# Attention kernel: probability-value products at two places of a step instead of three, and the causal mask of two maxima units moved from TensorE to VectorE

## What is computed

```python
scores = jnp.einsum('bshd,bthd->bhst', q, k) / jnp.sqrt(HEAD_DIM)
causal = jnp.tril(jnp.ones((S, S), dtype=bool))[None, None]
scores = jnp.where(causal, scores, -jnp.inf)
probs = jax.nn.softmax(scores, axis=-1)
out = jnp.einsum('bhst,bthd->bshd', probs, v).reshape(B, S, KEY_DIM)
```

## Time and profile before

| | us |
|---|---|
| median of 3 runs | 1171.12 |
| lowest, highest | 1170.22, 1174.72 |
| the profiled execution | 1182.48 |
| its span, first to last instruction | 1179.3 |
| TensorE busy | 975.2 |
| VectorE busy | 620.9 |
| GpSimd busy | 464.2 |
| ScalarE busy | 446.0 |

### The profile page before, as it was taken

How to read it: one execution, slowest core, us unless ns; L and a number is a source line. 1 busy time by engine, 2 the same in 40 slices (tenths; PEclk the granted TensorE clock), 3 DMA queues, 4 the chain that set the end, 5 groups by cost and what they waited for, 6 DMA issues and landing times. The chain is left out here.

```text
span 1179.3 us, 17823 instructions
## 1 busy us (share of the span) xinstructions
PE 975.2 (83%) x6250; PEld 773.6 (66%) x6250; DVE 620.9 (53%) x1802; ACT 446.0 (38%) x800; POOL 464.2 (39%) x432
## 2 busy tenths in 40 slices
PE   3699999887419999999943489899999739999996
PEld 1466767564319999999941256575666427888885
DVE  5666787956513333333335767776666143353534
ACT  0155555443003333333300045555556314433332
POOL 3453544464523333222345243454243415434232
PEclk9799999897659999999985689999999659999998
DMA  3442212010142323332022552423310010000001
GB/s 129 160 149 95 81 54 92 26 50 10 63 173 95 112 90 111 116 115 94 22 83 69 187 170 77 160 87 112 126 55 28 1 46 1 1 2 18 18 1 36
DMA packets 50023, 91.78 MB, mean 78 GB/s; under 512 B 7328, under 2 KB 22944, under 8 KB 49824
## 3 DMA queue, kind: packets, MB, share of 16 engines
q1 hardware_dynamic: 46880, 82.49, 20.8%
q0 software_dynamic: 3072, 8.39, 2.2%
HBM read 54.55 MB, written 36.31 MB: 77 GB/s over the span
## 5 line engine op out<-in xcount | busy, mean ns | idle before, releaser
L746 ACT ACTIVATE a_probs<-a_ps_b 128x512 f32<-128x512 f32 x320 | 188.1, 600 | 190.2 <-PE a_ps_b L810 186.4
L794 PE MATMUL a_ps_a<-a_k_st,a_q_st 128*128 128x256 f32 (+3 forms) x512 | 204.2, 440 | 26.9 <-DMA a_k_st<-scratch 17.3
L1004 DVE CUSTOM_DVE_ANT_0 a_masked_s<-a_ps_a,a_mask_f 128x512 f32<-128x512 f32 (+1 forms) x256 | 155.2, 621 | 86.6 <-PE a_ps_a L794 80.6
L794 PEld LDWEIGHTS a_ps_a<-a_k_st,a_q_st 128*128 128x128 f32 x512 | 102.5, 203 | 89.6 <-issue 42.6
L475 POOL TENSOR_SCALAR_AFFINE_SELECT a_probs<-a_probs 128x512 f32<-128x512 f32 x128 | 80.9, 646 | 198.3 <-ACT a_probs L746 198.0
L1594 POOL TENSOR_TENSOR w_lo<-w_raw,w_hi 128x2048 fp32r<-128x2048 f32 x16 | 73.9, 4616 | 186.7 <-ACT w_hi L1612 186.7
L810 PE MATMUL a_ps_b<-a_q_less,a_k_st 128*128 128x384 f32 (+3 forms) x512 | 140.2, 337 | 3.0 <-ACT a_probs L746 2.1
L810 PEld LDWEIGHTS a_ps_b<-a_q_less,a_k_st 128*128 128x128 f32 x512 | 91.3, 197 | 28.6 <-ACT a_probs L746 17.8
L1620 ACT ACTIVATE exp_h_hi<-exp_ps_u 128x320 fp32r<-128x320 f32 x128 | 49.2, 437 | 148.4 <-PE exp_ps_u L1684 148.4
L834 PE MATMUL a_ps_pv<-a_probs,a_v 128*32 128x512 f32 (+3 forms) x1024 | 94.9, 470 | 10.7 <-POOL a_probs L475 10.7
L1649 DVE SCALAR_TENSOR_TENSOR exp_h_lo<-exp_ps_u,exp_h_hi 128x320 fp32r<-128x320 f32 x128 | 56.8, 485 | 69.5 <-ACT exp_h_hi L1620 69.5
(11 more groups left out here) (238 smaller groups left out, 2296.2 us busy)
## 6 DMA issues: line engine op xcount, KB each, us to landing
w_raw<-in_m_w SPq DMA_DIRECT2D x16, 1024.0 KB, 5.1
scratch<-a_hi SPq DMA_DIRECT2D x24, 512.0 KB, 2.8
scratch<-a_lo SPq DMA_DIRECT2D x24, 256.0 KB, 3.1
a_q_st<-scratch SPq DMA_DIRECT2D x64, 96.0 KB, 2.6
a_k_st<-scratch SPq DMA_DIRECT2D x64, 96.0 KB, 2.6
...
```

Source lines behind the costliest of these rows:

```text
L746: nc.scalar.activation(probs[:, k, :], ps_b[k % B_BANKS][:, :], ACT.Exp, scale=scale).then_inc(exps, 1)
L794: last = nc.tensor.matmul(ps[:, at:at + wd], q_st[t % STACKS][:, h // PER_TILE, i * P:wd], k_st[t % STACKS][:, h, 0:wd], start=True, stop= ...
L1004: nc.vector.tensor_tensor_reduce(masked_s[n % 2][:, 0:wd], ps[:, 0:wd], mask_f[:, SEQ - wd:SEQ], -1.0, -NEG, ALU.add, ALU.min, nmax[:, t % ...
```

## The change

In `max_unit` the products of units 8 and 9 lose their mask product; unit 10 keeps it. In `unit_max` units 8 and 9 are read by two `tensor_tensor_reduce` of 256 columns, one per head, in place of one `tensor_reduce` over both; they wait for the use of `masked_s` two units ago, as units 0 to 7 do. `pv(t, 0)` moves from place 9 of T = t + 1 to place 2 of T = t + 2, ahead of `pv(t, 1)` and `pv(t, 3)`, behind a wait for three `masked` in place of one.

```diff
                 for h, i, at in max_work(k):
                     wd = (i + 1) * P
                     last = nc.tensor.matmul(ps[:, at:at + wd], q_st[t % STACKS][:, h // PER_TILE, i * P:wd],
-                                            k_st[t % STACKS][:, h, 0:wd], start=True, stop=(k < 8),
+                                            k_st[t % STACKS][:, h, 0:wd], start=True, stop=(k < 10),
                                             skip_group_check=True)
-                    if k >= 8:
+                    if k == 10:
                         last = mask(ps, at + i * P)
                 last.then_inc(a_full, 1)
...
                     if s == 2 and 0 <= T - 2 < STEPS:
+                        if (T - 2) % GROUPS == 0:
+                            emptied(pe, ("v", (T - 2) // GROUPS, 0))
+                            emptied(pe, ("v", (T - 2) // GROUPS, 1))
                         pe.wait_ge(masked, (T - 2) * 4 + 3)
+                        need(pe, pv_copied, T - 2)
+                        pv(T - 2, 0).then_inc(pv_done, 1)
                         pv(T - 2, 1)
                         pv(T - 2, 3).then_inc(pv_done, 1)
                     if s == 5 and 0 <= T - 2 < STEPS:
                         pe.wait_ge(masked, (T - 2) * 4 + 4)
                         pv(T - 2, 2).then_inc(pv_done, 1)
-                    if s == 9 and 0 <= T - 1 < STEPS:
-                        if (T - 1) % GROUPS == 0:
-                            emptied(pe, ("v", (T - 1) // GROUPS, 0))
-                            emptied(pe, ("v", (T - 1) // GROUPS, 1))
-                        pe.wait_ge(masked, (T - 1) * 4 + 1)
-                        need(pe, pv_copied, T - 1)
-                        pv(T - 1, 0).then_inc(pv_done, 1)
...
                 if k < 10:
-                    out, src = nmax[:, t % 2, 1, 2 * (k - 8):2 * (k - 8) + 2], ps[:, :].rearrange("p (h n) -> p h n", h=2)
-                else:
-                    out, src = nmax[:, t % 2, 0, :], ps[:, :].rearrange("p (h n) -> p h n", h=HPG)
-                nc.vector.tensor_reduce(out, src, AX_X, ALU.max, negate=True).then_inc(a_free, 1)
+                    dve.wait_ge(a_free, n - 1)
+                    for h, i, at in max_work(k):
+                        last = nc.vector.tensor_tensor_reduce(masked_s[n % 2][:, at:at + 2 * P], ps[:, at:at + 2 * P],
+                                                              mask_f[:, SEQ - 2 * P:SEQ], -1.0, -NEG, ALU.add, ALU.min,
+                                                              nmax[:, t % 2, i, h:h + 1])
+                    last.then_inc(a_free, 1)
+                    return
+                nc.vector.tensor_reduce(nmax[:, t % 2, 0, :], ps[:, :].rearrange("p (h n) -> p h n", h=HPG), AX_X, ALU.max,
+                                        negate=True).then_inc(a_free, 1)
```

## The result

The changed kernel took 1168.66 us (median of 20 runs, 1165.07 to 1173.37), the kernel before 1174.15 beside it (1169.63 to 1181.99). The ratio is 0.9946, 95% interval 0.9931 to 0.9962, a gain of 6.3 us by the ratio and 5.5 by the two medians, where 11.3 were forecast. Measured again on another chip the ratio was 0.9925 (0.9904 to 0.9946), 8.8 us. So the sign and the range held, and the size did not: the measured gain is half to three quarters of the sum. What failed are three terms for single groups of steps (the four partly covered ones, the nine late ones and step 13 of layer 0): together they were forecast at +3.5 us and came to +9.8.

A forecast was written before the change was run, and what follows sets the result against it. TensorE was taken to set attention's pace, with VectorE possibly late at `less`. Terms -8.5 - 2.0 - 2.4 + 7.3 - 3.0 - 1.8 - 0.9 = -11.3 us, off the 1171.1 median, gave 1160 us, range 1149 to 1174.

The forecast's parts named there:

- four partly covered ones: Four attention steps with part of the VectorE idle time and slack before `less`: about -0.5 us each, -2.0 together.
- nine late ones: Layer 0 steps 8, 9, 12, 15, layer 1 steps 2, 5, 6, 9, 15: VectorE solid to the end, +7.3 us together.
- step 13 of layer 0: Clock at half, `pv` takes 1.94 us in place of 1.07, and VectorE waited for the unit behind it: -1.8 us.
- Start and step 1: First two steps of each phase: -0.7 and -1.6 us in layer 0, -0.3 and +0.2 in layer 1, together -2.4.
- the full steps: Twelve steps with enough VectorE idle time and slack before `less` gain the full 0.71 us each: -8.5 us.
- the waits for GpSimd: Steps 8 and 12 of layer 1, where `pv(t, 0)` waited for GpSimd's mask: about -1.5 us each, -3.0 together.
- The ends: Ends of the two phases: about -1.4 us in layer 1 and +0.5 in layer 0, -0.9 in the sum.
- TensorE's saving per step, 0.71 us: On TensorE each step: 0.48 us from masks of units 8 and 9, 0.23 from two `pv` places instead of three.
- VectorE's new form: Two 256-column reductions in units 8 and 9, 0.34 us each by starts: 0.1 us more a unit, 0.2 a step.
- The rival of the clock: Longer waits at `less` drop the clock in five late layer 1 steps, about 4 us each: +9, 1180 us; chance 0.16.
- Taking 11.3 from the profile to the median: The 11.3 us gain, summed from the 1182.48 us profiled execution, was subtracted from the median: 1171.1 - 11.3 = 1159.8.

The follow-up runs named there:

- mixed kernel: Changed kernel, but steps 8, 9, 12, 13, 15 of layer 0 and 1, 2, 5, 6, 9, 15 of layer 1 as before: 1159.29 us, ratio 0.9869.
- late masks on TensorE: Changed kernel, but eleven steps listed as late keep the masks of units 8 and 9 on TensorE; product moved everywhere: 1172.35 us, ratio 0.9906 to before.
- block 0 ahead with masks on TensorE: Kernel before with block 0's product moved to place 1, ahead of `less`, in every step; all masks on TensorE: 1160.62 us, ratio 0.9838.
- the three products ahead of `less`: Changed kernel, but products of blocks 0, 1 and 3 at place 1, ahead of `less`: 1165.73 us, 0.9847 of before; again 1170.33 us, 0.9911.

## Why the prediction was right and wrong, step by step

The terms of the sum that failed are the second, the fourth and the sixth of the table: the partly covered steps (-2.0, measured 0.0), the nine late steps (+7.3, measured +9.3) and step 13 of layer 0 (-1.8, measured +0.5). Start and step 1 gave 0.5 us less than forecast; the full steps, the waits for GpSimd and TensorE's prices held. The ends (-0.9) came to -4.4 and -5.0, by nothing that the forecast named: this is luck, and it hides about half of the miss in the steps. Behind the late steps stands the clock, which the forecast had as a rival and put into no term.

- **TensorE's saving per step, 0.71 us:** right, 0.78 to 0.80 in the steps without a late engine. The masks came to 0.50 (sized at 0.48), the two places instead of three to 0.29 (sized at 0.23), each measured alone.
- **VectorE's new form:** the price was right (0.35 us a start for 0.34), its reach was not. With the product at its old place it makes step 3 of layer 1 late, and costs 3.5 to 6 us in all.
- **Which steps are late:** eight of nine did not gain, as forecast. In layer 0 steps 8, 9 and 12 stay as long as before (+0.08, -0.04, +0.02), step 15 pays 1.80. In layer 1 steps 2, 5, 6 and 15 pay 1.74, 2.01, 3.04 and 1.06; step 9 paid nothing (-0.45). The mixed kernel confirms the list as a whole. The masks alone do not make all of them late: with those alone steps 8, 9 and 12 of layer 0 and 9 of layer 1 are 0.48 to 0.51 us shorter in both profiles; with the move alone they change by -0.28 to +0.12. The term was +7.3 and measured +9.3: 1.05 was taken as the most a step can pay, and four paid 1.7 to 3.0, the three of layer 1 with a fall of the clock in or right behind the step. That the total is only 2.0 off is luck in part, since three steps of layer 0 and one of layer 1 paid nothing.
- **The partly covered steps:** -2.0 forecast, 0.0 measured. Steps 6 and 10 came right (-0.53, -0.46). Step 2 (+0.53, +0.54 in the second profile) was late. Step 14 (+0.42, +1.17) begins in a stretch at 0.50, and it is also a step that came out 2.5 us longer with unchanged code.
- **Step 13 of layer 0:** the clearest miss, -1.8 forecast, +0.5 measured, in both profiles. The slow `pv` did go away. But VectorE is held by GpSimd's long instruction, its routing and the maxima of unit 9 queue behind, and TensorE, which has come to this place with less work left, waits 5.47 us. After, timeline of all engines:

```profile
221.92 4.53 POOL L610 TENSOR_TENSOR w_lo<-w_raw,w_hi 128x2048 fp32r<-128x2048 f32 x1 [1.66 <-ACT w_hi L760]
...
222.77 3.77 DVE L1150 SCALAR_TENSOR_TENSOR a_slot<-a_top_atf,a_rank 128x4 f32<-128x4 f32 x2
...
229.78 1.11 PE L884 MATMUL a_ps_m<-kept_ident,kept_sub 128*128 128x128 f32 x4 [5.47 <-DVE kept_sub L1039]
```

  The hold is not new. In the kernel before the same instruction of GpSimd held another one of VectorE, and for longer (it takes 0.41 us elsewhere):

```profile
225.81 4.52 POOL L610 TENSOR_TENSOR w_lo<-w_raw,w_hi 128x2048 fp32r<-128x2048 f32 x1 [1.65 <-ACT w_hi L760]
225.95 4.53 DVE L1089 TENSOR_SCALAR kept_sub<-kept_x,kept_mean,kept_rstd 128x256 f32<-128x256 f32 x1
```

  TensorE's waits in the step were 2.60 and 2.37 us then, for two other products, so it waits no less than before. The Trainium skill ("SBUF — State Buffer", section "SBUF: two separate sides") says that of a VectorE instruction with two inputs from SBUF and one of GpSimd that reads SBUF, the first to start blocks the other for the whole instruction; the rows of after agree. I had priced the wait that goes, and not asked where the hold falls once TensorE and VectorE come there at another moment. The experiments say that in this step the two halves of the change don't add up: with the product moved and the masks still on TensorE the step is 2.91, 2.86 and 3.00 us shorter (the move alone, late masks on TensorE, block 0 ahead with masks on TensorE), more than the 1.8 of the sum. With the masks off TensorE as well it is 0.50 longer with them on VectorE and 0.32 longer with none; and without the move it is 0.58 shorter with them on VectorE, 0.33 and 0.21 longer with none. In the move alone VectorE is held for less time, and TensorE waits 1.84 us for the same `kept_sub`:

```profile
225.13 2.49 DVE L1145 SCALAR_TENSOR_TENSOR a_slot<-a_top_atf,a_rank 128x4 f32<-128x4 f32 x2
```

- **GpSimd's waits in steps 8 and 12 of layer 1:** right, -1.86 and -1.33 for two times -1.5. The wait of 2.91 us in front of the last product is down to 0.8 us, but moving that product alone is worth nothing (1.0015).
- **The rival of the clock** (0.16, "each such drop about 4 us, it decides from three on"): the mechanism was real and the price too high. Drops came at 695 to 705, 710 to 720 and 760 to 775 us in layer 1 and one at 210 to 215 in layer 0 (before: 700 to 710 in layer 1), and those of layer 1 cost the 8.3 us estimated above, 6 more than before's and under 3 each. It took a good half of the forecast gain and not all of it. The evidence I used against it, the clock of 1.00 in 800 to 850 us, was read in the one stretch of layer 1 with few late steps; there it is still 1.00.
- **Taking 11.3 from the profile to the median:** both profiled executions are long ones, and the stretches outside attention move by 5 us from one to the next. The steps themselves show 3.4 and 2.5, the ratios 6.3 and 8.8. The other 3 to 6 us lie outside the steps. In the second profile they are behind the last `less` (7.5 us shorter, clock 0.74 against 0.60); the twelve traces with the move make it likely that this belongs to the change, but it is not shown, and moving the last product alone does not bring it.

What stays open: why the masks alone give so little (0.9995, 0.9968) when every full step is 0.5 us shorter with them, while their 0.1 to 0.3% and the 0.5% of the move alone do add up to the change within the intervals; why in layer 1 the steps 1, 5 and 6 lengthen even with no masks and no move (by 0.7, 0.3 and 1.1 us in the second trace), which less work on TensorE alone does not explain; why the clock behind the last `less` is higher with the move; and the two values of the three products ahead of `less`. The clock in a step, and now and then a wait, differs from one execution to the next, and the traces at hand don't part this from the kernels.
